# Weight loads on one queue, a single gate buffer, and an early first qkv load in an eight-core linear-attention layer

## The reference, cut to what matters

```python
x = hidden_states                                  # (8, 2048, 2048) f32
xn = layernorm(x)
# branch 1: lightning attention, 16 heads of 128, blocks of 256
qkv  = silu(xn @ w_qkv.T)                          # w_qkv (6144, 2048)
for each head: scan over 8 blocks
    o_inter = (q * q_decay) @ kv
    o_intra = ((q @ k.T) * diag_decay) @ v
    kv      = block_decay * kv + (k * k_decay).T @ v
out  = norm_w * (out * rsqrt(mean(out * out) + 1e-6))
gate = sigmoid(xn @ w_gate.T)
s    = (gate * out) @ w_out.T
# branch 2: a linear layer whose weight is built from 4 bit planes
soft   = sigmoid(pweight) - sigmoid(nweight)       # (2048, 2048, 4) each
weight = einsum('oin,n->oi', soft, exps * sigmoid(mask_weight)) * scale
g = silu(xn @ weight.T + bias)
return x + s * g
```

## Time and profile before

| | us |
|---|---|
| median of the runs shown (2447.2 and 2456.6) | 2451.9 |
| the profiled execution | 2462.7 |
| its span on core 6, the slowest | 2460.5 |
| spans of the eight cores | 2435.4 to 2460.5 |
| PE busy | 1638.4 |
| DVE busy | 867.4 |
| ACT busy | 559.0 |
| POOL busy | 149.8 |
| q0, POOL's DMAs: 88.09 MB | 28.4% of 16 engines |
| q1, SP's DMAs: 143.17 MB | 18.0% of 16 engines |

### The profile page before, as it was taken

The page is one execution under the profiler, slowest core; times in us unless marked ns, Lnnn a source line. Parts: engine busy times, 40 slices in busy tenths (PEclk is TensorE's granted clock), DMA queues, the critical chain, the costliest instruction groups (busy, mean ns, idle before and its releaser), DMA issues.

```text
span 2460.5 us, 22651 instructions; the slowest of 8 cores (2435.4 to 2460.5 us)
## 1 busy us (share of the span) xinstructions
PE 1638.4 (67%) x7928; PEld 765.5 (31%) x7928; DVE 867.4 (35%) x1613; ACT 559.0 (23%) x827; POOL 149.8 (6%) x228
## 2 busy tenths in 40 slices
PE   1110543543558999288888888888888887367896
PEld 1110211221223444043434444343343343123342
DVE  5555244444541000213333333333333333624455
ACT  2225355544543112411111111111111111000000
POOL 0002222111110000000000000000000000110000
PEclk9999777776778999699999999999999999579998
DMA  6219899999992111412221112222222200697555
GB/s 162 103 52 120 127 156 192 197 202 216 209 205 71 39 39 39 71 26 43 43 44 32 30 27 41 43 43 44 43 44 43 43 18 9 135 185 167 162 166 151
DMA packets 176703, 232.70 MB, mean 95 GB/s; under 512 B 74064, under 2 KB 123216, under 8 KB 172496
## 3 DMA queue, kind: packets, MB, share of 16 engines
q0 software_dynamic: 124416, 88.09, 28.4%
q1 hardware_dynamic: 52176, 143.17, 18.0%
HBM read 277.37 MB, written 41.94 MB: 130 GB/s over the span
## 4 chain that ended last, share of the span: by engine, by line
PE 47%; DMA 25%; DVE 12%; issue 8%; ACT 5%; SPq 2%; POOL 0%; DVEq 0%; ACTq 0%; POOLq 0%
PE pfA L595 28%; DMA pnbg<-pwT 6%; DMA xT_fc<-xT 6%; DMA pnbg<-nwT 6%; PE pfA L465 4%; PE pS L465 4%; DMA pnq<-nwT 4%; ACT sq_b L740 2%; DVE sT_b L691 2%; PE pfA L352 2%; PE pT L627 2%; PE pS L352 1%; DVE mneg_c L195 1%; PE pT L243 1%; DVE s L932 1%
## 5 line engine op out<-in xcount | busy, mean ns | idle before, releaser
L595 PE MATMUL pfA<-xnT,wq_sb 128*128 128x512 bf16 x3072 | 724.3, 391 | 46.4 <-ACT q_dim L611 23.9
L595 PEld LDWEIGHTS pfA<-xnT,wq_sb 128*128 128x128 bf16 x3072 | 299.5, 101 | 406.8 <-issue 88.1
L352 PE MATMUL pfA<-xnT,wg_sb 128*128 128x512 bf16 x512 | 142.7, 448 | 333.0 <-ACT gate_stA L362 143.7
L691 DVE TENSOR_TENSOR sT_b<-pS,decT_all 128x512 bf16<-128x512 f32 x128 | 88.3, 690 | 320.7 <-PE pS L679 320.7
L418 DVE TENSOR_TENSOR sgp<-sgp,sgn 128x1024 bf16<-128x1024 bf16 x128 | 88.5, 692 | 292.6 <-ACT sgn L414 292.6
L352 PEld LDWEIGHTS pfA<-xnT,wg_sb 128*128 128x128 bf16 x512 | 56.1, 112 | 419.2 <-issue 379.5
L748 DVE SCALAR_TENSOR_TENSOR O_st<-pO,csb,gate_h 128x256 bf16<-128x256 f32 x128 | 61.8, 483 | 308.7 <-ACT sq_b L740 307.1
L409 ACT ACTIVATE sgp<-pnbg 128x1024 bf16<-128x1024 bf16 x128 | 134.1, 1048 | 113.5 <-DMA pnbg<-pwT 108.9
L917 PE MATMUL pfA<-O_sb,wout_sb 128*128 128x512 bf16 x512 | 129.6, 413 | 42.1 <-DVE s L926 42.1
L243 PE MATMUL pT<-id_bf,xntok 128*128 128x128 bf16 x256 | 29.8, 309 | 147.0 <-DVE xntok L232 147.0
L430 DVE SCALAR_TENSOR_TENSOR Wacc<-sgp,cpos,Wacc 128x1024 f32<-128x1024 bf16 x96 | 123.2, 1284 | 10.3 <-DVE sgp L418 0.5
(11 more groups left out here) (109 smaller groups left out, 1455.1 us busy)
## 6 DMA issues: line engine op xcount, KB each, us to landing
pnq<-nwT SPq DMA_DIRECT2D x80, 512.0 KB, 9.9
pnbg<-pwT POOLq DMA_DIRECT2D x128, 256.0 KB, 12.9
wq_sb<-wqkvT POOLq DMA_DIRECT2D x16, 1536.0 KB, 15.8
xtile<-x SPq DMA_DIRECT2D x16, 1024.0 KB, 6.1
xT_fc<-xT SPq DMA_DIRECT2D x16, 1024.0 KB, 8.1
outT<-outb SPq DMA_DIRECT2D x64, 256.0 KB, 3.2
pnbg<-nwT POOLq DMA_DIRECT2D x48, 256.0 KB, 13.1
wg_sb<-wgateT POOLq DMA_DIRECT2D x16, 512.0 KB, 19.8
```

The source lines that it names most:

```text
L352: r = e.matmul(pbank[:], wg_sb[b][:, fc * HD:(fc + 1) * HD], xnT[:, fc * T + tg * 512: fc * T + tg * 512 + 512], start=(fc == 0), stop=(fc ...
L595: r = e.matmul(pfA[par][:], wq_sb[hb][:, fc * 384 + sel * 128: fc * 384 + (sel + 1) * 128], xnT[:, fc * T + tg * 512: fc * T + tg * 512 + ...
L691: tst = sch.op("V", (lambda h, jp: lambda e: e.tensor_tensor(out=sT_b[:, jp * 512:(jp + 1) * 512], in0=pS[jp][:], in1=decT_all[:, h * 512: ...
```

## The change

The `nwT` halves of all 128 units go by POOL into the four bf16 buffers; `SPLIT_UI`, the three `pnq` buffers and the SP loads are gone. There is one `gate_st`; its store follows its head's sigmoids at once, and the next head's first sigmoid waits for it. The first qkv weight has a buffer of its own, `wq_sb0`, outside the stages, and its load is the first DMA of POOL, with no wait.

```diff
     t_cst = sch.op("Q", lambda e: e.dma_start(out=csb[:], in_=consts_ap),
                    inc=True, sem="cst")
+    tok_wq0 = sch.op("G", lambda e: e.dma_start(
+        out=wq_sb0[:].rearrange("p (c j) -> p c j", j=384),
+        in_=wqkvT_ap[0].rearrange("(c p) j -> p c j", p=128)),
+        inc=True, sem="wq0")
...
+    wq_sb0 = esABC.enter_context(nc.sbuf_tensor("wq_sb0", [128, NFC * 384], BF16))
...
-    pnq = [esPN.enter_context(nc.sbuf_tensor(f"pnq{i}", [128, D // 2], F32))
-           for i in range(3)]
-    SPLIT_UI = 48
...
-        gate_st = [sbB("gate_stA", (128, T), BF16), sbB("gate_stB", (128, T), BF16)]
+        gate_st = [sbB("gate_stA", (128, T), BF16)]
...
-            gb = h % 2
+            gb = 0
...
-                    waits=[tok_gmm[(h, tg)], tok_gsd.get(h - 2)], inc=True)
-        def emit_gsd(h):
-            gb = h % 2
+                    waits=[tok_gmm[(h, tg)], tok_gsd.get(h - 1)], inc=True)
             tok_gsd[h] = sch.op("Q", (lambda h, gb: lambda e: e.dma_start(
                 out=gate_dram[h], in_=gate_st[gb][:]))(h, gb),
-                waits=[tok_gst[h * NTG + NTG - 1]], inc=True, sem=f"gsd{h % 2}")
+                waits=[tok_gst[h * NTG + NTG - 1]], inc=True, sem="gsd0")
...
+                    bq = 4 + ui % 4
...
-                    if ui < SPLIT_UI:
-                        bn = 4 + ui % 4
...
-                    else:
-                        bq = ui % 3
-                        nbuf = pnq[bq]
-                        tok_pn[(ui, 1)] = sch.op("Q",
...
-                            waits=[tok_sig.get((ui - 3, 1))],
-                            inc=True, sem=f"pq{bq}")
+                    tok_pn[(ui, 1)] = sch.op("G",
+                        (lambda ic, n, hf, bq: lambda e: e.dma_start(
+                            out=pnbg[bq][:],
+                            in_=nwT_ap[n, ic * 128:(ic + 1) * 128,
+                                       hf * HD2:(hf + 1) * HD2]))(ic, n, hf, bq),
+                        waits=[tok_sig.get((ui - 4, 1))],
+                        inc=True, sem=f"pn{bq}")
...
-            emit_gsd(step)
...
-        wq_sb = [sbC(f"wq_sb{i}", (128, NFC * 384), BF16) for i in range(2)]
+        wq_sb = [wq_sb0, sbC("wq_sb1", (128, NFC * 384), BF16)]
...
-        tok_wq[0] = sch.op("G", lambda e: e.dma_start(
-            out=wq_sb[0][:].rearrange("p (c j) -> p c j", j=384),
-            in_=wqkvT_ap[0].rearrange("(c p) j -> p c j", p=128)),
-            waits=tok_ffn_done + [tok_gsd[NH - 1]], inc=True, sem="wq0")
+        tok_wq[0] = tok_wq0
```

More of the change, by code:

```diff
@@ L413, in emit_pn_chunk @@
                     tok_sig[(ui, 1)] = sch.op("S",
-                        (lambda ui, nbuf, sp: lambda e: e.activation(
-                            out=sgn[sp][:], in_=nbuf[:], func=AF.Sigmoid))(ui, nbuf, sp),
+                        (lambda ui, bq, sp: lambda e: e.activation(
+                            out=sgn[sp][:], in_=pnbg[bq][:], func=AF.Sigmoid))(ui, bq, sp),
                         waits=[tok_pn[(ui, 1)], tok_comb.get((ui - 2, 0))], inc=True)
```

## The result

The changed kernel takes a median of 2437.9 us (12 runs) against 2464.8 us (11 runs) for the kernel before, run beside it. The ratio is 0.9901 with a 95% interval of 0.9877 to 0.9925, so about 24 us or 1% faster: a difference clear of the noise, and less than 2%. One run of the changed kernel and two of the other, 3 to 9% longer than the rest, are left out of the ratio and not of the medians, which lie 27 us apart. The profiled execution took 2434.9 us against 2462.7.

What follows compares the result with a forecast made beforehand. Transfers were taken to bind the stretch making WffnT's 16 chunks. From the 2451.9 us median, 20 for the queue and 0 for the other parts gave 2431.9, called 2432; 8-in-10 range 2412 to 2462.

Steps and rivals of the forecast that it cites:

- The signs named in advance: Signs of being right: last cast near 728 us, first FFN matmul near 744, ACT's first q_dim eviction near 1019.
- The stretch that binds, and the price of a chunk: Transfer-bound making of WffnT: chunks 6 to 15 take 32.8 us for 35.0; 20 us gained, ends 7.5 and 33.
- The reason given: WffnT chunks: of two queues' streams now one, now the other is late; one queue holds transfers in order of use.
- One gate_st: Gate stores: the wait is hidden behind a chunk's sigmoids, except heads 14 and 15; 0 us, ends 0 and +6.
- wq_sb0 early: After the FFN: 19 us already hidden by decay tables, 0 (-19 to 0); at the start 0 (-4.2 to +15.8).
- Rival B: WffnT chunks: bytes read bind, early chunks quick only with cores in step; intervals stay 35.0, 2452 us; chance 0.15.
- Rival C: WffnT chunks: wg_sb's wait for a head's last matmul stops the single POOL queue; interval 37.9, 2481 us; chance 0.08.
- Rival D: Qkv start after the FFN: the early wq_sb0 does bring its 19 us, giving 2413 us; chance 0.05.
- Rival E: WffnT chunks: DVE's hold on POOL is exposed, 3 us x 10 = 30 above the forecast, 2462 us; chance 0.10.

## Why the prediction was right

The forecast was 20 us less, and 2432 us; the measurement says 24 less (18 to 30 by its interval), and 2437.9 us. The level is off because 2451.9, the median of the two runs shown, lies below ten of the eleven runs of that kernel; the difference is what was forecast. The signs named in advance came, on core 6: cast 15 at 727.8 (728), the first FFN matmul at 743.4 (744), the first q_dim eviction at 1019.4 (1019). The steps by their own order:

- *The stretch that binds, and the price of a chunk.* Right. 32.8 us was taken from the three one-queue chunks of the trace before; the changed kernel gave 326.8/10 = 32.7. The forecast for the mean core was -22, measured -23.2. The -20 was a middle between that and core 6's own 17.6; core 6 gained 22.7 in the stretch. A slow core's early chunks did not foretell its late ones: core 0, with 7.5 us expected, gained 25.4. The mean over the cores was the better estimator. That core 6 would stay the slowest did not hold: it is core 0 in this execution, and it differs from run to run.
- *The reason given.* Half right. One queue is what counts; buffers, bytes written and f32 packets are not, and transfers bind afterwards. That it must be in the order of use was not tested, as no run put one queue in another order. And I read the loss as two streams drifting apart in general. Most of it, 18 of 23 us, hangs on the wg_sb load in one of them, which the forecast named, for this term, only as equal work in both regimes. The number did not suffer, because the price was read from whole chunks that held this load too, whatever the reason; the reason alone would have misled in a kernel without it.
- *One gate_st.* 0 foretold; cast 15 to the FFN is 20.2 us for 20.5. Right.
- *wq_sb0 early.* 0 foretold at both ends, and right. TensorE starts 3.2 us behind the FFN and stands until ACT comes, which is at 53.8 us (53.9 before). At the start DVE waits 3.5 to 4.4 us for x tiles on the eight cores (3.6 to 5.5 before); the slowest core:

```profile
DVE mneg_c L197 <- DMA xtile<-x: 4.4, 3, 2.2
```

and TensorE and ACT between the FFN and head 0, to be read beside the earlier trace rows:

```profile
950.01 7.07 PE L452 MATMUL pS<-xnT,WffnT 128*128 128x512 bf16 x32
961.38 8.75 PE L579 MATMUL pfA<-xnT,wq_sb 128*128 128x512 bf16 x32 [4.30 <-DMA g_scr<-g_st]
1012.70 1.86 PE L579 MATMUL pfA<-xnT,wq_sb 128*128 128x512 bf16 x4 [42.57 <-ACT q_dim L595]
...
1011.96 1.09 ACT L595 ACTIVATE q_dim<-pfA 128x512 bf16<-128x512 f32 x2
```

- *Rival B, no gain,* fell: all eight cores gained in the stretch, 12 to 29 us. *Rival C, POOL stopped at the load,* fell: no such wait in the steady part. *Rival D* fell by the run with the late load. *Rival E, VectorE's hold,* fell by its price, and not because the stall is absent. On core 0 none of the 128 issues of L383 took over 0.605 us, but on core 5 one did:

```profile
210.36 1.23 DVE L424 CAST WffnT<-Wacc 128x2048 bf16<-128x2048 f32 x1
210.38 1.32 POOL L383 DMA_DIRECT2D pnbg<-pwT  x1 [1.60 <-ACT sgp L397]
```

The trace of the changed kernel thus shows the stall that the Trainium skill ("SBUF — State Buffer", "SBUF: two separate sides") describes: the issue begins within the cast and ends some 0.12 us behind it, as the one of the earlier trace rows did (212.45 behind 212.32). It is the only one of the 2048 issues of pwT and nwT on the eight cores that took over 0.7 us, so its price here is near nothing. The forecast says that the three all-POOL chunks show the stall; its row, at 210.93, stands before their stretch (298.7 to 398.4 on core 6). Within it the stall is found on core 1, once: an issue of L392 at 297.19 takes 1.01 us beside the multiplication that is L424 in the kernel before (297.33 to 298.09).

## What to carry to other kernels

In this kernel, where two weight streams are consumed in turn and the transfers bind, one queue in the order of use beat two queues by 1% of the time, though the second had its own buffers. Most of that needs a third load in one of the two queues; without it the difference was 5 us, too little to tell from scatter. So look first for the load that stands in only one of the queues. Where a kernel has both regimes in one trace, the mean over the chunks and all the cores gives the price of the change, better than the slowest core alone did here. A load moved early buys nothing while another chain ends later at the same place: shorten that chain first.

## What the runs showed that I had not expected

A fourth buffer for nwT hardly shortened the waits but moved them, to 110 to 135 us for pwT. A fifth buffer on one queue lengthened the landing from 12.9 to 18.5 us and brought no time. The split cost 2.6 to 4.1 us a chunk among chunks 3 to 5 and 2.3 among the later ones; whether the early ones really suffer more is open. The ACT operations with a scale per partition take 0.49 to 0.51 us for 256 columns and 0.70 for 512, where those with a constant take 0.42 and 0.63, but they need no VectorE between them. And the cores end 30 us apart in the profiled execution of the changed kernel, and up to 49 in others of the kernel before, though each does the same work; from the last qkv matmul to the end they need 369 to 388 us in the changed kernel, and which core is slow there changes from run to run.
